# A graph attention kernel on Trainium2: SyncE fetches three search stretches out of four, one row a transfer, and GpSimd keeps the fourth

## The chip, the cores and the metric

One NeuronCore of one Trainium2 chip runs the whole kernel in one launch. The metric is the device time of one execution in microseconds (us). Engines carry the profile's short names: PE is TensorE, DVE is VectorE, ACT is ScalarE, POOL is GpSimd, SP is SyncE. SP has no arithmetic: it issues transfers (DMA) and waits. A name with a q (SPq) is the sequencer of that engine.

## The reference, cut to what matters

```python
h = x @ w_lin + b_lin                     # 12500 nodes, 64 features
msg = h[edge_src]                         # 400000 edges, sorted by edge_dst
counts = segment_sum(ones, edge_dst)      # edges of each node
starts = cumsum(counts) - counts          # where a node's edges begin
pos = arange(e) - starts[edge_dst]
dense[edge_dst, pos] = msg                # (12500, 32, 64), further edges dropped
mask[edge_dst, pos] = True
xb = mab(dense, dense, enc_*, mask)       # attention of a node's 32 slots among themselves
xp = relu(xb @ pma_lin_w + pma_lin_b)
p = mab(seed, xp, pma_*, mask)            # pooling to one vector a node
dd = mab(p, p, dec_*)                     # decoder
out = layernorm(x + relu(nan_to_num(dd)))
```

## The kernel before

**Work.** A slot is one of a node's 32 edges, a quad is 32 partitions, an octet is 32 nodes with their 1024 slots. There are 391 octets. Four octets are one iteration of 128 nodes, and there are 98 iterations (ITS). First a table of 12500 rows of 192 numbers (what the query, the feature and the value of a node come from) is computed and stored in DRAM as `node_table`; then the octets go through a software pipeline. All engines run `step(s)` for each octet number, written out for the first 16 steps, as a loop of 22 turns of PERIOD = 16 steps, and written out again for the tail. What an engine does in a step for an older or a younger octet is said by a lag (`L_FF = 4`: the octet four steps back; `AT_SEARCH = -6`: six steps ahead).

**Gathers.** In each step POOL issues eight indirect transfers at L547, each of which fetches 128 table rows into `gathered`, at the row numbers in `idx`. `gathered` has a ring of 8 octets; a step's gathers wait for `av_ps`, the attention product of the octet eight back. PE waits with L639 for the gathers of its octet.

**Search.** `idx` is found on the chip. For each iteration, DVE counts in `rows_of` (step lag AT_ROWS = -15) how many of 1250 samples of the sorted edge list lie below each of the 128 nodes (L908, `count_rows`), which gives for each node the row of `win_table` at which its edges begin. A row of `win_table` is a stretch of 352 edge targets and the same 352 edge sources, 2816 bytes. At lag AT_STRETCH = -8 POOL fetches the 128 rows of one iteration into `windows[:, buffer]` in one indirect transfer, `gather_windows` (L510), ahead of the step's eight gathers. At lag AT_SEARCH = -6 DVE waits for it in `landed`, and counts and shifts in the stretch in place; at lag -4 it writes `idx`. So the row numbers of an iteration are known seven steps before its stretch is fetched, and nine before it is searched. The first four iterations (DIRECT) are fetched another way, L517. There are two stretch buffers.

**SP.** SP loads inputs, stores the table, builds `win_table` (L476, L479), and then waits in L488 for the output parts, which are ready at the end. It does nothing between 67 us and 3919 us.

Of the kernel before, what the change touches and what calls it, by code (L numbers as in the profile page):

```python
# [25 lines left out]
ALU = mybir.AluOpType  # L26
# [22 lines left out]
STAGED = 16  # L49
DIRECT = 4  # L50
PERIOD = 16

# [26 lines left out]
class Step:  # L79
# [15 lines left out]
    def round(self, lag):  # L95
        return self.group * (PERIOD // RING) + (self.at - lag) // RING

    def slot(self, lag, n):
# [28 lines left out]
def gnn_kernel(nc, a, out):  # L127
# [33 lines left out]
    with ExitStack() as ctx:  # L161
# [19 lines left out]
        empty = sb("empty", [P, 512])  # L181
        consts = sb("consts", [P, 512])
        probs = sb("probs", [P, 2, 512])
# [34 lines left out]
        iota_j = sb("iota_j", [P, DEG])  # L218
        iota_ji = sb("iota_ji", [P, DEG], I32)
        node_i = sb("node_i", [P, ITS], I32)  # L220
        node_f = sb("node_f", [P, ITS])
# [21 lines left out]
        def c_(n, rows_=D):  # L243
# [4 lines left out]
        sample_i = sb("sample_i", [SAMPLE_ROWS, SAMPLE_TILES], I32)  # L248
        sample_f = sb("sample_f", [SAMPLE_ROWS, SAMPLE_TILES])
        sample_diag = xp_rows[0:SAMPLE_ROWS, :, :].rearrange("p s n -> p (s n)")[  # L250
            :, 24 * D:24 * D + SAMPLES].rearrange("p (k r) -> p k r", k=SAMPLE_TILES)
        ones = sb("ones", [SAMPLE_ROWS, P])
# [60 lines left out]
        x_in = [sem(f"x_in{i}") for i in range(6)]  # L313
        win_in = [sem(f"win_in{i}") for i in range(2)]
        found = sem("found")
# [64 lines left out]

        pe_passed, pool_passed, dve_passed = sem("pe_passed"), sem("pool_passed"), sem("dve_passed")

        block = ctx.enter_context(nc.Block())
# [62 lines left out]
        def _(sp):  # L446
# [35 lines left out]


            stores = 0
            for part, (lo, end) in enumerate(PARTS):
# [10 lines left out]
        def _(pool):  # L496
# [10 lines left out]
            one_where_zero(ident[:, :], [[-1, P]], 0)  # L507
            def gather_windows(u, buffer, at):
                wait_apart(pool, win_idx_ready, u - (DIRECT - 1), pool_passed)
                pool.indirect_dma_start(  # L510
                    out=windows[:, buffer, 0:2 * WIN], out_offset=None, in_=win_table,
                    in_offset=bass.IndirectOffsetOnAxis(ap=win_idx[:, at:at + 1], axis=0)).then_inc(win_in[buffer], 16)

            def gather_direct(u):
                pool.wait_ge(win_elem_ready, u + 1)
                for c, edges in enumerate((dst, src)):
                    pool.indirect_dma_start(  # L517
                        out=windows[:, u % 2, c * WIN:(c + 1) * WIN], out_offset=None,
                        in_=edges.rearrange("(n o) -> n o", o=1),
                        in_offset=bass.IndirectOffsetOnAxis(ap=win_elem[:, u:u + 1], axis=0)).then_inc(win_in[u % 2], 16)  # L520

# [6 lines left out]
            def step(s):  # L528
# [3 lines left out]
                if not s.looped and s.at in (0, 12 + AT_STRETCH):  # L532
                    u = 2 + (s.at > 0)
                    pool.wait_ge(idx_ready, u - 1)
                    gather_direct(u)
# [21 lines left out]
        def _(pe):  # L557
# [18 lines left out]
            for lo in range(0, SAMPLES, 512):  # L576
                hi = min(lo + 512, SAMPLES)
                pe.matmul(ps_samples[:, lo:hi], ones[:, :], flat[:, lo:hi], start=True, stop=True
                          ).then_inc(samples_ps, 1)
# [256 lines left out]
        def _(dve):  # L836
# [11 lines left out]
            V.memset(pma_diag[:, :], 0.0).then_inc(dve_zero, 1)  # L848
            V.memset(ones[:, :], 1.0)
            V.memset(consts[:, :], 0.0)  # L850
# [74 lines left out]

            def landed(u, half):

                direct = 2 if not isinstance(half, int) else min(half + 1, 2)
                dve.wait_ge(win_in[u], half * 16 + (16 + 16 * direct))

# [49 lines left out]
            for c in range(CHUNKS):  # L980
                table_odd(c)
                if c in (2, 4, 6):
                    elements_of(c // 2)
                if c == 8:
                    landed(0, 0)
                    search(0, 0, 0, 0)
                if c == 12:
                    landed(1, 0)
# [46 lines left out]

            iota_slots = iota_j[:, :].unsqueeze(1).broadcast_to((P, 2, DEG))

            def step(s):
# [135 lines left out]
                if s.has_iteration(AT_SEARCH) and (s.looped or s.at >= 8 + AT_SEARCH):  # L1174
                    u = s.iteration(AT_SEARCH)
                    par = s.slot(AT_SEARCH, RING) // OCTS_PER_IT
                    landed(par, s.round(AT_SEARCH))
                    count_edges(u, par, par)
                    shift(u, par, range(BITS - 1, SHIFTS - 1, -1))
                if s.has_iteration(AT_SHIFT) and (s.looped or s.at >= 8 + AT_SHIFT):  # L1180
                    par = s.slot(AT_SHIFT, RING) // OCTS_PER_IT
                    shift(s.iteration(AT_SHIFT), par, range(SHIFTS - 1, -1, -1))
# [3 lines left out]
                    index_of(par, s.slot(AT_SHIFT, PERIOD) // OCTS_PER_IT)  # L1186
                if s.has_iteration(AT_ROWS) and (s.looped or s.at >= 4 * DIRECT + AT_ROWS):
                    rows_of(s.iteration(AT_ROWS), s.slot(AT_ROWS, PERIOD) // OCTS_PER_IT)

# [93 lines left out]
```

## Time and profile before

| | |
|---|---|
| time, median of 3 runs | 4168.89 us (4167.66 to 4169.9) |
| the profiled execution | 4176.05 us, its span 4174.2 us |
| POOL | 3067.2 us busy, 73% of the span, 3236 instructions |
| PE | 3126.7 us, 75% |
| DVE | 3035.1 us, 73% |
| ACT | 1659.8 us, 40% |
| gathers L547 | 3125 |
| stretch gathers L510 | 94 |

Busy time counts executing alone. An engine whose instructions each need a fixed pause of issue behind them can be fully taken at 73% busy, so for each engine the reader has to look at what its idle time waited for. The span holds about 67 us of preparation, the pipeline, and a drain behind the last gather at 4108 us.

### The profile page before, as it was taken

How to read it: one execution, taken by the hardware profiler on the slowest of the kernel's cores; microseconds unless marked ns; L12 is line 12 of the kernel's file. 1: busy time of each engine (PE TensorE's matmuls, PEld its weight loads, DVE VectorE, ACT ScalarE, POOL GpSimd, SP SyncE). 2: the span in 40 equal slices, each digit the busy share in tenths (PEclk: the TensorE clock that was granted, in tenths of full speed). 3: DMA queues.
4: the chain of work that ended last, by engine and by line, in shares of the span. 5: the costliest groups of instructions: out<-in, count | busy, mean ns of one | idle time of the engine just before them, and what ended most of it. 6: DMA issues, size and time to landing. Idle time of an engine off the chain costs nothing.

```text
span 4174.2 us, 87208 instructions
## 1 busy us (share of the span) xinstructions
PE 3126.7 (75%) x30724; PEld 2000.1 (48%) x30724; DVE 3035.1 (73%) x7088; ACT 1659.8 (40%) x2990; POOL 3067.2 (73%) x3236
## 2 busy tenths in 40 slices
PE   5677777777777777777777777777777777777776
PEld 3444444454444444444444454444444444444444
DVE  4677777777777777777777777777776777777876
ACT  2343443444434434443444343443443444434443
POOL 3777777777777777777777777777777777777772
PEclk7898999999999999999999999999999999999998
DMA  5333333333333333333333333333333333333331
GB/s 197 87 85 88 85 88 84 87 88 85 87 86 87 85 88 85 87 85 88 85 87 86 87 85 88 85 87 85 88 87 85 88 85 87 85 88 85 97 95 35
DMA packets 170668, 368.55 MB, mean 88 GB/s; under 512 B 56190, under 2 KB 109094, under 8 KB 170230
## 3 DMA queue, kind: packets, MB, share of 16 engines
q0 software_dynamic: 158032, 342.73, 30.7%
q1 hardware_dynamic: 11877, 19.76, 1.3%
q8 instruction: 289, 4.73, 0.5%
q14 instruction: 150, 1.22, 0.1%
q10 hardware_dynamic: 320, 0.10, 0.0%
HBM read 349.58 MB, written 16.32 MB: 88 GB/s over the span
## 4 chain that ended last, share of the span: by engine, by line
POOL 63%; issue 21%; PE 7%; DMA 4%; DVE 3%; POOLq 1%; ACT 0%; SPq 0%; ACTq 0%; DVEq 0%
POOL gathered L547 61%; DMA gathered<-node_table,idx 4%; POOL windows L510 2%; PE ps L724 2%; PE ps L651 2%; PE ps L697 2%; DVE xb L1119 1%; PE ps L639 1%; DVE probs_diag L1193 0%; DVE flags L908 0%; POOLq L122 0%; PE ps L606 0%; POOLq L124 0%; PE ps L752 0%; DVE h L1075 0%
## 5 line engine op out<-in xcount | busy, mean ns | idle before, releaser
L547 POOL DMA_INDIRECT gathered<-node_table,idx x3125 | 2969.4, 950 | 952.4 <-issue 934.4
L639 PE MATMUL ps<-ident,gathered 128*128 128x128 f32 x3128 | 608.0, 326 | 748.7 <-DMA gathered<-node_table,idx 748.4
L639 PEld LDWEIGHTS ps<-ident,gathered 128*128 128x128 f32 x3128 | 501.7, 204 | 1104.8 <-issue 1062.8
L803 ACT ACTIVATE qT<-ps,cols 128x512 f32<-128x512 f32 x391 | 268.9, 688 | 1238.8 <-PE ps L639 1237.8
L1119 DVE SCALAR_TENSOR_TENSOR xb<-ps,cols,h 128x512 f32<-128x512 f32 x391 | 292.6, 748 | 640.6 <-PE ps L697 640.0
L761 ACT ACTIVATE h_apart<-ps 64x512 f32<-64x512 f32 x782 | 462.8, 592 | 443.7 <-PE ps L639 434.1
L1193 DVE STREAM_TRANSPOSE probs_diag<-probs 32x512 f32<-32x512 f32 x784 | 549.0, 700 | 18.3
L697 PE MATMUL ps<-h,ff_diag 128*128 128x512 f32 x782 | 505.6, 734 | 29.8 <-DVE h L1075 29.7
L651 PE MATMUL ps<-probs_diag,gathered 128*64 128x128 f32 x6256 | 449.4, 287 | 79.0 <-issue 78.6
L651 PEld LDWEIGHTS ps<-probs_diag,gathered 128*64 128x64 f32 x6256 | 363.3, 167 | 247.4 <-issue 230.9
L724 PE MATMUL ps<-xb,pma_diag 128*128 128x512 f32 x782 | 454.4, 664 | 31.3 <-DVE xb L1119 26.9
L683 PE MATMUL ps<-xp,seed_u 128*32 128x128 f32 x3128 | 431.1, 283 | 0.0
L761 ACT ACTIVATE xp_rows<-ps 128x512 f32<-128x512 f32 x391 | 233.5, 597 | 416.2 <-PE ps L675 415.6
L683 PEld LDWEIGHTS ps<-xp,seed_u 128*32 128x32 f32 x3128 | 318.7, 112 | 72.9 <-issue 68.8
L1075 DVE SCALAR_TENSOR_TENSOR h<-ps,cols,hT 128x512 f32<-128x512 f32 x391 | 290.5, 743 | 35.3 <-PE ps L651 35.3
L816 ACT ACTIVATE xp<-ps,cols 128x512 f32<-128x512 f32 x391 | 267.8, 685 | 97.7 <-PE ps L724 95.7
L961 DVE COPY_PREDICATED windows<-below_bits,windows 128x128 int32<-128x128 int32 (+8 forms) x882 | 211.9, 240 | 94.9 <-DVE windows L961 55.2
L675 PE MATMUL ps<-ident,xp 128*128 128x128 f32 x1564 | 252.5, 286 | 7.5 <-ACT xp L816 1.1
L761 ACT ACTIVATE hT<-ps 128x512 f32<-128x512 f32 x391 | 233.6, 597 | 9.8
L740 PEld LDWEIGHTS ps<-h_apart,qT 128*32 128x32 f32 x12544 | 189.7, 110 | 77.5 <-issue 76.0
L724 PEld LDWEIGHTS ps<-xb,pma_diag 128*128 128x128 f32 x782 | 122.9, 198 | 211.0 <-DVE xb L1119 106.2
L740 PE MATMUL ps<-h_apart,qT 128*32 128x64 f32 x12544 | 221.2, 222 | 1.5 <-ACT h_apart L761 1.4
(195 smaller groups left out, 3369.3 us busy)
## 6 DMA issues: line engine op xcount, KB each, us to landing
gathered<-node_table,idx POOLq DMA_INDIRECT x3125
node_table<-gathered SPq DMA_DIRECT2D x24, 384.0 KB, 2.8
out_rows<-rows SPq DMA_DIRECT2D x5, 416.0 KB
win_table<-in_dst SPq DMA_DIRECT2D x1, 1716.0 KB
win_table<-in_src SPq DMA_DIRECT2D x1, 1716.0 KB
windows<-win_table,win_idx POOLq DMA_INDIRECT x94, 3.7
rows<-in_x SPq DMA_DIRECT2D x2, 640.0 KB, 5.2
rows<-in_x SPq DMA_DIRECT2D x1, 768.0 KB, 7.2
```

The source lines that it names most:

```text
L547: pool.indirect_dma_start(out=gathered[:, s.slot(0, RING), t * ROW:(t + 1) * ROW], out_offset=None, in_=table, in_offset=bass.IndirectOffs ...
L639: mm = pe.transpose(ps[:, bank, p * P:(p + 1) * P], gathered[:, s.slot(0, RING), lo:lo + 2 * ROW - 2:3], ident[:, :])
L651: mm = pe.matmul(ps[D * h:D * h + D, B_AV, p * P:(p + 1) * P], gathered[:, s.slot(L_ATTEND, RING), lo:lo + ROW - 2:3], probs_diag[:, s.slo ...
L683: mm = pe.matmul(ps_seed[DEG * c:DEG * c + DEG, :], seed_u[:, 6 - 2 * p:38 - 2 * p], xp[:, s.slot(L_BACK, 2), p * P:(p + 1) * P], start=(p ...
L697: pe.matmul(ps[:, B_FF, :], ff_diag[:, :], h2[:, s.slot(L_FF, 2), :], start=True, stop=True).then_inc(ff_ps, 1)
L724: pe.matmul(ps[:, B_FF, :], pma_diag[:, :], xb[:, s.slot(L_PMA, 2), :], start=True, stop=True).then_inc(pma_ps, 1)
L740: mm = pe.matmul(ps[DEG * q:DEG * q + DEG, B_S + o, 2 * DEG * p:2 * DEG * (p + 1)], qT[:, s.slot(L_SCORES - o, 4), lo:lo + DEG], h_apart[: ...
L761: return nc.scalar.activation(o, i, ACT.Copy)
L803: nc.scalar.activation(qT[:, s.slot(0, 4), :], ps[:, B_Q, :], ACT.Identity, bias=c_("q_b", P)).then_inc(q_sb, 1)
L1075: V.scalar_tensor_tensor(h2[:, s.slot(L_H2, 2), :], ps[:, B_AV, :], c_("bo1", P), hT[:, s.slot(L_H2, RING), :], ALU.add, ALU.add).then_inc ...
L1119: V.scalar_tensor_tensor(xb[:, s.slot(L_FF, 2), :], ps[:, B_FF, :], c_("ff_b", P), h2[:, s.slot(L_FF, 2), :], ALU.add, ALU.max).then_inc(x ...
L1193: V.transpose(probs_diag[lo:lo + DEG, s.slot(L_NORM, 4) // 2, :, lo:lo + DEG], pr[lo:lo + DEG, :].rearrange("p (t j) -> p t j", j=DEG)).th ...
```

## The change

Of each four iterations, the one with `at == 0` is still fetched by POOL. The other three are fetched by SP: DVE transposes the column of 128 row numbers, so that the 32 numbers of a quad lie side by side in one partition (`odd_turned`); SP loads each quad's 32 numbers into registers, and issues for each a transfer of one row of `win_table` into one partition of `windows`. Each is a DMA with an address from a register. Four stretch buffers take the place of two, and DVE waits on four semaphores (one a quad) for a stretch of SP. To make room, `flags` are bf16 and some tiles share memory. In all 70 of the 94 stretches move to SP, in 23 turns of a loop of three stretches and one more behind it, and all ahead of the output stores in SP's order.

```diff
@@ sync
+            def odd_rows(b, count):
+
+                wait_apart(sp, odd_turned_ready, count, sp_passed)
+                for q in range(QUADS):
+                    _, at = nc.values_load_multi_w_load_instructions(
+                        odd_turned[DEG * q:DEG * q + 1, b, :], engines=(mybir.EngineType.SP,), min_val=0,
+                        max_val=SAMPLES - 1, skip_runtime_bounds_check_because="a count of the samples, less one")
+                    for j in range(DEG):
+                        sp.dma_start(windows[DEG * q + j:DEG * q + j + 1, 1 + b, 0:2 * WIN],
+                                     win_table[bass.ds(at[j], 1), :]).then_inc(odd_in[b][q], 16)
+
+            sp.wait_ge(table_in, 64)
+            with sp.Fori(0, (ITS - 6) // 4) as turn:
+                for k in range(3):
+                    odd_rows(k, turn * 3 + k + 1)
+            odd_rows(0, (ITS - 6) // 4 * 3 + 1)
@@ gpsimd
-            def gather_windows(u, buffer, at):
-                wait_apart(pool, win_idx_ready, u - (DIRECT - 1), pool_passed)
+            def gather_windows(s):
+                wait_apart(pool, win_idx_ready, s.period(AT_STRETCH), pool_passed)
+                at = s.slot(AT_STRETCH, PERIOD) // OCTS_PER_IT
                 pool.indirect_dma_start(
-                    out=windows[:, buffer, 0:2 * WIN], out_offset=None, in_=win_table,
-                    in_offset=bass.IndirectOffsetOnAxis(ap=win_idx[:, at:at + 1], axis=0)).then_inc(win_in[buffer], 16)
+                    out=windows[:, 0, 0:2 * WIN], out_offset=None, in_=win_table,
+                    in_offset=bass.IndirectOffsetOnAxis(ap=win_idx[:, at:at + 1], axis=0)).then_inc(win_in[0], 16)
@@ gpsimd, step
-                if s.has_iteration(AT_STRETCH) and (s.looped or s.at >= 16 + AT_STRETCH):
+                if s.has_iteration(AT_STRETCH) and s.slot(AT_STRETCH, PERIOD) == 0 and (s.looped or s.at >= 16 + AT_STRETCH):
                     wait_apart(pool, idx_ready, s.iteration(AT_STRETCH) - 1, pool_passed)
                     if not s.looped and s.at == 16 + AT_STRETCH:
                         pool.wait_ge(table_in, 64)
-                    at = s.slot(AT_STRETCH, PERIOD) // OCTS_PER_IT
-                    gather_windows(s.iteration(AT_STRETCH), at % 2, at)
+                    gather_windows(s)
@@ vector
-            def rows_of(u, at):
-
+            def rows_of(s):
+
+                u = s.iteration(AT_ROWS)
+                at = s.slot(AT_ROWS, PERIOD) // OCTS_PER_IT
                 count_rows(u, at, u + 1)
-                V.tensor_scalar(win_idx[:, at:at + 1], win_row[:, at:at + 1], -1.0, None, ALU.add).then_inc(win_idx_ready, 1)
+                minus = V.tensor_scalar(win_idx[:, at:at + 1], win_row[:, at:at + 1], -1.0, None, ALU.add)
+                if at == 0:
+                    minus.then_inc(win_idx_ready, 1)
+                else:
+                    n = s.period(AT_ROWS) * 3 + (at - 3)
+                    minus.then_inc(odd_idx_ok, 1)
+                    wait_apart(dve, odd_idx_ok, n, dve_passed)
+                    V.transpose(odd_turned[:, at - 1, :], win_idx[:, at:at + 1].broadcast_to((P, DEG))
+                                ).then_inc(odd_turned_ready, 1)
@@ vector, landed(s)
+                at = s.slot(AT_SEARCH, PERIOD) // OCTS_PER_IT
+                if at:
+                    for q in range(QUADS):
+                        dve.wait_ge(odd_in[at - 1][q], s.period(AT_SEARCH) * (16 * DEG))
+                else:
+                    dve.wait_ge(win_in[0], s.period(AT_SEARCH) * 16 + 32)
+                return at
@@ memory
-        windows = sb("windows", [P, 2, 2 * WIN + DEG], I32)
+        windows = sb("windows", [P, 4, 2 * WIN + DEG], I32)
-        flags = [sb(f"flags{i}", [P, n]) for i, n in enumerate((SAMPLES, WIN, WIN))]
+        flags = [sb(f"flags{i}", [P, n], BF16) for i, n in enumerate((SAMPLES, WIN, WIN))]
```

On POOL, this stands before in the first eight of the 16 steps of the loop (`L122` is a register instruction of a wait; eight gathers are one step; line numbers here are those of the file before):

```order
L122 REGISTER_ALU
L510 DMA windows<-win_table,win_idx 128x704
L122 ISA
L547 DMA gathered<-node_table,idx 128x192 x8
L122 REGISTER_ALU
L547 DMA gathered<-node_table,idx 128x192 x8
L122 REGISTER_ALU
L547 DMA gathered<-node_table,idx 128x192 x8
L122 REGISTER_ALU
L547 DMA gathered<-node_table,idx 128x192 x8
L122 REGISTER_ALU x2
L510 DMA windows<-win_table,win_idx 128x704
```

In the changed kernel (where L571 is the gather and L537 the stretch gather) the only stretch gather of POOL's loop stands behind the eighth step of a turn:

```order
L571 DMA gathered<-node_table,idx 128x192 x8
L126 REGISTER_ALU
L571 DMA gathered<-node_table,idx 128x192 x8
L126 REGISTER_ALU x2
L537 DMA windows<-win_table,win_idx 128x704
L126 REGISTER_ALU
L571 DMA gathered<-node_table,idx 128x192 x8
```

So a turn of 16 steps has 128 gathers and one stretch gather on POOL, where it had 128 and four.

On SP, the transfers that build `win_table` (L488 here) are followed by the new loop, whose L505 is its head, L497 the load of 32 row numbers into registers, each ISA at L501 the address arithmetic of one row, and each DMA at L501 one row:

```order
L488 DMA win_table<-in_src 2x352
L505 UNCONDITIONAL_BRANCH
L505 ISA
L497 TENSOR_LOAD odd_turned
L501 ISA
L501 DMA windows<-win_table 1x704
L501 ISA
L501 DMA windows<-win_table 1x704
```

Before, the output stores followed directly there. Now a stretch is four loads and 128 pairs of ISA and DMA, and the stores stand behind the last stretch.

## Rows read from the trace of the kernel before

**Rows 1.** The page: span, busy time, and the chain that ended last.

```profile
span 4174.2 us, 87208 instructions
...
PE 3126.7 (75%) x30724; PEld 2000.1 (48%) x30724; DVE 3035.1 (73%) x7088; ACT 1659.8 (40%) x2990; POOL 3067.2 (73%) x3236
...
POOL 63%; issue 21%; PE 7%; DMA 4%; DVE 3%; POOLq 1%; ACT 0%; SPq 0%; ACTq 0%; DVEq 0%
POOL gathered L547 61%; DMA gathered<-node_table,idx 4%; POOL windows L510 2%; PE ps L724 2%; PE ps L651 2%; PE ps L697 2%; DVE xb L1119 1%; PE ps L639 1%; DVE probs_diag L1193 0%; DVE flags L908 0%; POOLq L122 0%; PE ps L606 0%; POOLq L124
```

**Rows 2.** Waits of POOL: us in total, times, longest us.

```profile
POOL gathered L547 <- issue: 934.4, 3066, 0.3
POOL windows L510 <- issue: 28.6, 94, 0.3
POOL gathered L547 <- PE ps L651: 18.0, 59, 0.3
```

**Rows 3.** Timeline of POOL: start us, us, what, idle before it.

```profile
2010.56 0.95 POOL L510 DMA_INDIRECT windows<-win_table,win_idx  x1 [0.31 <-issue]
2011.81 0.95 POOL L547 DMA_INDIRECT gathered<-node_table,idx  x1 [0.30 <-issue]
```

**Rows 4.** Lines L510, L547: count, ns min/median/max, first and last start.

```profile
L510 POOL DMA_INDIRECT windows<-win_table,win_idx x94: 942/947/1031, 150.5 to 3999.3; - x94
...
L547 POOL DMA_INDIRECT gathered<-node_table,idx x3125: 942/947/1892, 67.8 to 4108.4; - x196
```

**Rows 5.** Busy time of each engine in 16 steps of the loop.

```profile
core 0: us, PE busy (x) PEld busy (x) DVE busy (x) ACT busy (x) POOL busy (x), PEclk, DMA share, GB/s
2010.50:2176.00 165.50, 124.89 (x1244) 80.61 (x1244) 121.67 (x285) 66.79 (x120) 125.30 (x132) 0.93 0.32 86
```

**Rows 6.** Waits of all engines: PE for the gathers.

```profile
PE ps L639 <- DMA gathered<-node_table,idx: 748.4, 321, 10.1
```

**Rows 7.** Line L953 on VectorE, a transpose of 128x32.

```profile
L953 DVE STREAM_TRANSPOSE count_turned<-count x98: 198/203/329, 30.9 to 4037.9; 128x32 f32<-128x32 f32 x98
```

**Rows 8.** Issues of SP by line, ns min/median/max.

```profile
L488 SPq DMA_DIRECT2D out_rows<-rows x8: 332/332/357, 3919.1 to 4171.6; - x8
...
L453 SPq DMA_DIRECT2D rows<-in_x x5: 371/432/529, 3.9 to 5.8; - x5
...
L464 SPq DMA_DIRECT2D node_table<-gathered x24: 325/532/2212, 19.5 to 60.8; - x24
...
L479 SPq DMA_DIRECT2D win_table<-in_dst x1: 659/659/659, 63.7 to 63.7; - x1
L479 SPq DMA_DIRECT2D win_table<-in_src x1: 2011/2011/2011, 65.0 to 65.0; - x1
```

**Rows 9.** Timeline of SP: three issues.

```profile
59.69 0.53 SPq L464 DMA_DIRECT2D node_table<-gathered  x1
60.27 0.47 SPq L460 DMA_DIRECT2D cols<-in_L_gnn_dec_out_b  x1
60.84 0.53 SPq L464 DMA_DIRECT2D node_table<-gathered  x1
```

**Rows 10.** Sequencer instructions by line, ns min/median/max.

```profile
L908 DVEq FUSED_REGOPS  x88: 46/53/57, 260.6 to 3858.8; - x88
...
L389 PEldq COMPARE_BRANCH  x22: 83/3688/4318, 404.8 to 3879.5; - x22
...
L124 POOLq EVENT_SEMAPHORE  x616: 17/17/17, 218.1 to 3846.4; - x154
```

**Rows 11.** DMA queues: packets, MB, share of 16 DMA engines.

```profile
q0 software_dynamic: 158032, 342.73, 30.7%
q1 hardware_dynamic: 11877, 19.76, 1.3%
```

**Rows 12.** Waits of SP: us in total, times, longest us.

```profile
SPq L488 <- DVE rows L1256: 4102.2, 8, 3852.1
```

More of the change, by code:

```diff
@@ L50 @@
 DIRECT = 4
+DIRECT_BUFFER = (0, 1, 2, 3)
 PERIOD = 16
@@ L96, in round, with period @@
         return self.group * (PERIOD // RING) + (self.at - lag) // RING
+    def period(self, lag):
+        return self.group + (self.at - lag) // PERIOD
     def slot(self, lag, n):
@@ L181, in gnn_kernel @@
         empty = sb("empty", [P, 512])
-        consts = sb("consts", [P, 512])
+        consts = sb("consts", [P, 2 * P])
         probs = sb("probs", [P, 2, 512])
@@ L248, in gnn_kernel @@
         sample_i = sb("sample_i", [SAMPLE_ROWS, SAMPLE_TILES], I32)
-        sample_f = sb("sample_f", [SAMPLE_ROWS, SAMPLE_TILES])
+        sample_f = lnv[0:SAMPLE_ROWS, 0, 0:SAMPLE_TILES]
         sample_diag = xp_rows[0:SAMPLE_ROWS, :, :].rearrange("p s n -> p (s n)")[
             :, 24 * D:24 * D + SAMPLES].rearrange("p (k r) -> p k r", k=SAMPLE_TILES)
-        ones = sb("ones", [SAMPLE_ROWS, P])
-        flags = [sb(f"flags{i}", [P, n]) for i, n in enumerate((SAMPLES, WIN, WIN))]
+        ones = pool_part[0:SAMPLE_ROWS, 0:P]
+        flags = [sb(f"flags{i}", [P, n], BF16) for i, n in enumerate((SAMPLES, WIN, WIN))]
+        odd_turned = sb("odd_turned", [P, 3, DEG], I32)
         win_row = sb("win_row", [P, 4])
@@ L257, in gnn_kernel @@
         win_elem = sb("win_elem", [P, DIRECT], I32)
-        windows = sb("windows", [P, 2, 2 * WIN + DEG], I32)
+        windows = sb("windows", [P, 4, 2 * WIN + DEG], I32)
+        node_i = windows[:, 3, 0:ITS]
+        iota_ji = windows[:, 3, ITS:ITS + DEG]
         below = sb("below", [P, 1])
@@ L313, in gnn_kernel @@
         x_in = [sem(f"x_in{i}") for i in range(6)]
-        win_in = [sem(f"win_in{i}") for i in range(2)]
+        win_in = [sem(f"win_in{i}") for i in range(4)]
+        odd_in = [[sem(f"odd_in{b}{q}") for q in range(QUADS)] for b in range(3)]
+        odd_idx_ok = sem("odd_idx_ok")
+        odd_turned_ready = sem("odd_turned_ready")
         found = sem("found")
@@ L517, in gather_direct @@
                     pool.indirect_dma_start(
-                        out=windows[:, u % 2, c * WIN:(c + 1) * WIN], out_offset=None,
+                        out=windows[:, DIRECT_BUFFER[u], c * WIN:(c + 1) * WIN], out_offset=None,
                         in_=edges.rearrange("(n o) -> n o", o=1),
-                        in_offset=bass.IndirectOffsetOnAxis(ap=win_elem[:, u:u + 1], axis=0)).then_inc(win_in[u % 2], 16)
+                        in_offset=bass.IndirectOffsetOnAxis(ap=win_elem[:, u:u + 1], axis=0)).then_inc(win_in[DIRECT_BUFFER[u]], 16)
             for u in range(2):
@@ L577, in _ @@
                 hi = min(lo + 512, SAMPLES)
-                pe.matmul(ps_samples[:, lo:hi], ones[:, :], flat[:, lo:hi], start=True, stop=True
+                pe.matmul(ps_samples[:, lo:hi], ones, flat[:, lo:hi], start=True, stop=True
                           ).then_inc(samples_ps, 1)
@@ L848, in _ @@
             V.memset(pma_diag[:, :], 0.0).then_inc(dve_zero, 1)
-            V.memset(ones[:, :], 1.0)
+            V.memset(ones, 1.0)
             V.memset(consts[:, :], 0.0)
@@ L924, in elements_of, with direct_landed, landed @@
                                 ).then_inc(win_elem_ready, 1)
-            def landed(u, half):
-                direct = 2 if not isinstance(half, int) else min(half + 1, 2)
-                dve.wait_ge(win_in[u], half * 16 + (16 + 16 * direct))
+            def direct_landed(u):
+                b = DIRECT_BUFFER[u]
+                dve.wait_ge(win_in[b], 32 * DIRECT_BUFFER[0:u + 1].count(b))
+            def landed(s):
+                u = s.iteration(AT_SEARCH)
+                if not s.looped and u < DIRECT:
+                    direct_landed(u)
+                    return DIRECT_BUFFER[u]
+                at = s.slot(AT_SEARCH, PERIOD) // OCTS_PER_IT
[5 more added lines that the diff above has]
+                return at
             def search(u, h, buffer, at):
@@ L984, in _ @@
                 if c == 8:
-                    landed(0, 0)
+                    direct_landed(0)
                     search(0, 0, 0, 0)
                 if c == 12:
-                    landed(1, 0)
+                    direct_landed(1)
                     search(1, 1, 1, 1)
@@ L1036, in _ @@
             iota_slots = iota_j[:, :].unsqueeze(1).broadcast_to((P, 2, DEG))
+            searched = [0]
             def step(s):
@@ L1176, in step @@
                     par = s.slot(AT_SEARCH, RING) // OCTS_PER_IT
-                    landed(par, s.round(AT_SEARCH))
-                    count_edges(u, par, par)
-                    shift(u, par, range(BITS - 1, SHIFTS - 1, -1))
+                    searched[0] = landed(s)
+                    count_edges(u, par, searched[0])
+                    shift(u, searched[0], range(BITS - 1, SHIFTS - 1, -1))
                 if s.has_iteration(AT_SHIFT) and (s.looped or s.at >= 8 + AT_SHIFT):
-                    par = s.slot(AT_SHIFT, RING) // OCTS_PER_IT
-                    shift(s.iteration(AT_SHIFT), par, range(SHIFTS - 1, -1, -1))
+                    shift(s.iteration(AT_SHIFT), searched[0], range(SHIFTS - 1, -1, -1))
                     for lag in (12, 11, 10, 9):
@@ L1185, in step @@
                             dve.wait_ge(g_in[s.slot(lag, RING)], s.round(lag) * (16 * OCT) + 16 * OCT)
-                    index_of(par, s.slot(AT_SHIFT, PERIOD) // OCTS_PER_IT)
+                    index_of(searched[0], s.slot(AT_SHIFT, PERIOD) // OCTS_PER_IT)
                 if s.has_iteration(AT_ROWS) and (s.looped or s.at >= 4 * DIRECT + AT_ROWS):
-                    rows_of(s.iteration(AT_ROWS), s.slot(AT_ROWS, PERIOD) // OCTS_PER_IT)
+                    rows_of(s)
             def to_diagonal(s, pr, first, last):
```

7 lines of the change are left out of this document (2 added, 5 removed).

## The prediction

> **What bounds the kernel now.** I read the chain that ended last first. POOL's instructions are 63% of it and "issue" another 21%, nearly all of it the gathers of L547 [rows 1]. The waits of POOL say what that issue time is: 3066 of the 3125 gathers waited for nothing that the profile shows, 0.3 us each, and where PE's L651 is named, the wait is the same 0.3 us at most [rows 2]. The timeline shows the beat: a gather starts every 1.25 us, 0.95 executing and 0.30 of issue, and a stretch gather of L510 takes exactly one beat between two of them [rows 3]. So 73% busy is a full engine. From the first and last start of L510, 93 intervals of 33 beats lie in 3848.8 us [rows 4]: 41.385 us an iteration, **1.254 us a beat**, 165.5 us a turn of 16 steps (132 beats). In such a turn PE is busy 124.9 us and DVE 121.7 us [rows 5], and PE waits 748.4 us in all for landed gathers [rows 6], 1.9 us for each of 391 octets. The other engines have room; SP sleeps (its longest wait 3852.1 us [rows 12]).
>
> **What the change takes away.** 70 of the 94 beats of L510 leave POOL. 70 x 1.254 = **87.8 us**. A turn is then 129 beats, 161.8 us. The steps without a stretch gather already run at 8 beats, so nothing else is asked to be faster than it has been for three steps out of four.
>
> **What it adds on DVE.** For each of 70 stretches a 128x32 transpose, 0.20 us by the row of another one [rows 7], a wait of one DVE instruction for another (some 0.1 us) and three more semaphore waits: about 0.4 us, 1.2 us of a turn in which DVE has 40 free. It hides behind PE's wait for gathers [rows 6]; with that cover gone it would cost 70 x 0.4 = 28 us. bf16 flags change no count of instructions; I take nothing.
>
> **What it adds on SP, the term that decides.** A turn has three stretches: 384 row issues, each behind one fused register instruction, 12 register loads, a few waits, and one branch. The pieces:
> - Register instruction: 46 to 57 ns on DVE [rows 10]; I take 46.
> - The pause between two SP instructions: 60.27 - 59.69 - 0.53 = 0.05 us; with a semaphore wait in between, 60.84 - 60.27 - 0.47 = 0.10 [rows 9]. So 0.045 a pause, two a row. The row costs its issue + 0.136 us.
> - Register load of 32 words: no row. The nearest is a whole issue, 0.33 us [rows 8]; with its pause 12 x 0.375 = 4.5 us a turn. Below it is a register instruction (12 x 0.09 = 1.1); above I take one such instruction a word, 32 x 0.046 = 1.5 us, 18 us a turn.
> - Branch back: 3.7 us by PE's, whose loop is also long [rows 10]. Waits and counters: 0.5.
> - Sum: 384 x (issue + 0.136) + 8.7 us a turn.
>
> SP keeps up if this is below 161.8, that is **if an issue takes at most 0.263 us**; it costs more than before (165.5) above 0.272. Now the issues of the trace [rows 8]: alone, 128 rows on an idle SP, 0.325 to 0.332; close behind another 0.43 to 0.53; behind a transfer of 1248 rows 0.659 and 2.011. The last ones show that part of an issue grows with the size of the job ahead. None of the trace moves one row. An issue cannot be less than a semaphore instruction, 0.017 [rows 10], and the shortest seen is 0.325. The nearest row is the 0.33, with which SP would lose. I still take **0.25**: each of those issues starts 128 rows over all DMA engines, the new one starts a single contiguous piece, so that there is no job ahead to wait for and less to set up. That a quarter of 0.33 is such set-up is my choice, not a reading. With it a turn is 384 x 0.386 + 8.7 = **156.9 us**, 4.9 under POOL's 161.8, and SP is 97% taken. The first such stretch has nine steps (91 us) from its row numbers to its search; three in a row, at 52 us each, leave the third ready 157 - 80 = 77 us after its numbers, still early.
>
> The Trainium skill prices a register load as a "`tensor_load` floor" of about 600 ns (DMA: Bandwidth & Descriptors, Latency and other measured facts); by it, as an estimate, the loads are 7.7 us a turn in place of 4.5, and the sum is 160.1, just inside. No row here shows a load.
>
> **DMA.** The bytes are the same, 2816 a row. At the software queue's rate, 30.7% of 16 engines x 4174.2 us for 342.73 MB [rows 11], 59.8 us of one engine a MB, a row is 0.168 us; by the hardware queue's 1.3% for 19.76 MB it is 0.12. Spread over 16 engines that is nothing new. If all 128 rows went through one engine, it would have 21.5 us of them in 53.9 us, 40%, beside the 31% of the gathers: 71%. The gathers' landing may come a few tenths later; PE's 1.9 us an octet covers it. [...]
>
> **The drain.** The output stores stand behind the last stretch in SP's order. That stretch is needed by octet 388, some 9 steps before the pipeline's end, and seven of eight stores have no reader. Nothing.
>
> **Sum.** 4176.05 - 87.8 = 4088.3 for the profiled execution, which is 0.17% above the median; at the median 4168.9 - 87.8 = 4081. I say 4082.
>
> **Rivals.**
> - *SP becomes the bound, slower than before.* One mechanism: the issue of one row costs as much as that of 128. For it speaks that 0.325 is the shortest of all and the same at eight stores of different width. The end is then DVE waiting in `landed`, and behind it `idx`, POOL and PE. At 0.332 the turn is 384 x 0.468 + 8.7 = 188.4 us, 22.9 more than before, x 23.3 turns = +534: **4703**. At 0.30: 176.1, +247: 4416. At the 0.532 of back-to-back issues: 265.2, +2326: 6495. It decides from 0.272 us. Chance 0.29.
> - *Loads word by word.* With 0.25 for the issue but 1.5 us a load: 148.2 + 18.5 + 4.2 = 170.9, +5.4 a turn, +126: **4295**. It decides from 1.1 us a load. The Trainium skill gives some 200 ns a register for a load from HBM (Runtime: NRT & Kernel Launch, Instruction fetch mechanics); the estimate by it is 6.4 us a load and a turn of 229 us, 1480 us more. Chance 0.06.
> - *One DMA engine fills up.* If a row holds it for 0.35 us in place of 0.17, 128 x 0.35 + 16.7 = 61.5 us a stretch, 184.5 a turn, +443: **4612**. It decides from 0.30 us a row. Chance 0.03.
> - *Just at the edge.* An issue of 0.263 to 0.272: POOL's gain is eaten by SP, 4082 to 4169. Chance 0.05, 0.03 of it within the bound of no change.
> - *The forecast.* 4076 to 4092. Chance 0.57.
>
> **How the numbers follow.** Faster by over 0.2% (what can be told from no change here, 8 us): 0.57 + 0.02 = 0.59. Within: 0.03. Slower: 0.29 + 0.06 + 0.03 = 0.38. The cases lie on both sides. The range takes in the forecast, the edge, the word-by-word case, and the first rival up to its 0.332 us: 4075 to 4710; beyond it stay the dearer issues. The likeliest case's own range is 4076 to 4092.
>
> **What would show it.** Right: 24 stretch gathers on POOL, the beat still 1.25 us, POOL's waits still "issue", row issues of SP under 0.26 us, SP waiting for `odd_turned` a little in each stretch, and no wait of DVE at `landed`. Wrong: row issues at 0.3 us or more back to back without a wait of SP, long waits of DVE at the first count of a search (L941 before) for a transfer, POOL waiting for `idx`, and PE for it. A load longer than 1.1 us, or gathers that land later than before, would show the two smaller rivals.

## The result: slower by 12.3%

The changed kernel takes 4681.31 us (median of 4 runs, 4678.71 to 4682.61), the kernel before 4168.64 us on the same chip (4 runs, 4167.66 to 4169.9): a ratio of 1.1229, 95% interval [1.1209, 1.1248], 512.7 us more. The forecast of 4082 us is wrong in its sign; the time lies in the range, close to the first rival's 4703. The profiled execution took 4682.61 us.

The page of the changed kernel, with the chain that ended last and the queues, where [rows 1, 11] had POOL at 73% busy and 63% of the chain:

```profile
span 4680.8 us, 114667 instructions
...
PE 3046.6 (65%) x30724; PEld 1961.6 (42%) x30724; DVE 3044.4 (65%) x7158; ACT 1673.5 (36%) x2990; POOL 2992.1 (64%) x3166
...
q0 software_dynamic: 152432, 317.49, 25.7%
q1 hardware_dynamic: 29797, 45.03, 3.2%
...
SPq 68%; issue 26%; POOL 3%; PE 1%; DVE 1%; DMA 0%; ACT 0%; ACTq 0%; POOLq 0%; DVEq 0%
```

SP, which slept before, is 68% of the chain, and "issue" (mostly its own pauses) another 26%. The other engines do the work they did, in a longer span. POOL is 75 us less busy: 66 of them are the 70 stretch gathers that it lost (70 x 0.947), the other 9 are gathers of L571 that last 3 ns less in the mean. The two queues together take 28.9% of the DMA engines, where they took 32.0%. PE's mean granted clock fell from 0.912 to 0.855, but PE is busy 3046.6 us where it was 3126.7, so its matmuls did not get longer in sum.

What SP executes, by line of the changed kernel (L501 is the row's transfer, L497 the register load, L505 the loop; count, ns min/median/max, first and last start):

```profile
L501 SPq FUSED_REGOPS  x8960: 37/37/43, 141.7 to 4548.1; - x200
L501 SPq MOVE windows<-win_table x8960: 29/29/38, 141.8 to 4548.2; - x200
L501 SPq DMA_DIRECT2D windows<-win_table x8960: 224/225/304, 141.8 to 4548.2; - x200
...
L497 SPq TENSOR_LOAD <-odd_turned x280: 2029/2119/2291, 139.6 to 4532.9; - x140
...
L505 SPq ALU_OP  x23: 37/37/37, 325.9 to 4486.2; - x23
```

Three readings. The issue of one row is 0.225 us, below even the chosen 0.25. A load of 32 registers is 2.12 us, where the forecast had 0.33 (each with a pause behind it). And there is a third instruction a row, a MOVE, which the forecast did not have. The loop's counter instruction stands once in each of 23 passes: (4486.2 - 325.9) / 22 = **189.1 us a turn**, where POOL needs 161.8.

A stretch of SP's timeline (start us, us, what):

```profile
1701.57 4.35 SPq L501 DMA_DIRECT2D windows<-win_table  x11
```

Eleven rows, taken from the first one's MOVE to the last one's issue, last 4.35 us. Ten beats and the last row's MOVE, pause and issue (0.029 + 0.031 + 0.225) make that, so a row is 0.407 us. One such beat in the chain (start us, us, what): the issue of a row, the register instruction, the MOVE and the next issue, with a pause before each:

```profile
2000.17 0.23 SPq L501
2000.40 0.05 issue
2000.45 0.04 SPq L501
2000.48 0.04 issue
2000.52 0.03 SPq L501
2000.55 0.03 issue
2000.58 0.23 SPq L501
```

Who waits now (us in total, times, longest us):

```profile
PE ps L721 <- DVE h L1124: 1225.2, 227, 28.9
DVE flags L988 <- DMA windows<-win_table: 978.6, 45, 26.9
POOL gathered L571 <- issue: 939.1, 3080, 0.3
POOL gathered L571 <- DVE idx L1014: 460.0, 31, 22.2
...
PE ps L663 <- DMA gathered<-node_table,idx: 80.3, 25, 9.8
```

L988 is the first count of a search: DVE waits there for the rows, POOL waits for the `idx` that DVE then writes late, and PE's wait for gathers has shrunk from 748.4 us [rows 6] to 80.3, because PE now stands behind DVE instead (L721, 1225.2 us). SP itself waits for nothing but the start and the end:

```profile
SPq L514 <- DVE rows L1304: 124.8, 2, 111.4
SPq L128 <- DVE odd_turned L948: 59.0, 1, 59.0
```

One wait for row numbers in the whole execution, the first one. An engine whose input is always ready is the bound.

**The turn in pieces.** 384 rows x 0.407 = 156.3 us; 12 loads x 2.12 = 25.4; the rest of the 189.1, 7.4 us, is the pauses at loads and waits, the branch and longer pauses now and then. The largest single piece of it is the pause behind the branch back to the loop's head, once a turn:

```profile
2028.34 2.73 issue
```

### The profile page after: what moved, and what is told of

Its sections match the earlier page's. It is cut to its first block, busy times and chain, and to the rows that moved or that the text cites. A ratio compares the mean times of both kernels' runs of the same rounds, so it can differ in the third digit from the quotient of the medians.

```text
span 4680.8 us, 114667 instructions
## 1 busy us (share of the span) xinstructions
PE 3046.6 (65%) x30724; PEld 1961.6 (42%) x30724; DVE 3044.4 (65%) x7158; ACT 1673.5 (36%) x2990; POOL 2992.1 (64%) x3166
## 3 DMA queue, kind: packets, MB, share of 16 engines
q0 software_dynamic: 152432, 317.49, 25.7%
## 4 chain that ended last, share of the span: by engine, by line
SPq 68%; issue 26%; POOL 3%; PE 1%; DVE 1%; DMA 0%; ACT 0%; ACTq 0%; POOLq 0%; DVEq 0%
SPq L501 55%; SPq L497 12%; POOL gathered L571 3%; PE ps L630 0%; PE ps L721 0%; DVE flags L932 0%; PE ps L776 0%; DVE probs_diag L1241 0%; DVE windows L1008 0%; DVE gathered L1023 0%; DMA gathered<-node_table,idx 0%; PE ps L734 0%; PE ps L748 0%; PE ps L602 0%; PE ps L663 0%
## 5 line engine op out<-in xcount | busy, mean ns | idle before, releaser
L571 POOL DMA_INDIRECT gathered<-node_table,idx x3125 | 2960.7, 947 | 1403.4 <-issue 939.1
L721 PE MATMUL ps<-h,ff_diag 128*128 128x512 f32 x782 | 474.3, 691 | 1227.6 <-DVE h L1124 1225.2
L988 DVE TENSOR_SCALAR_CACHE_REDUCE flags<-windows,node_f 128x352 bf16<-128x352 int32 x98 | 55.8, 570 | 978.6 <-DMA windows<-win_table 978.6
L721 PEld LDWEIGHTS ps<-h,ff_diag 128*128 128x128 f32 x782 | 128.8, 207 | 1269.2 <-issue 1247.6
L663 PEld LDWEIGHTS ps<-ident,gathered 128*128 128x128 f32 x3128 | 468.3, 200 | 383.1 <-issue 382.2
L663 PE MATMUL ps<-ident,gathered 128*128 128x128 f32 x3128 | 554.6, 303 | 80.4 <-DMA gathered<-node_table,idx 80.3
```

The source lines that it names most:

```text
L571: pool.indirect_dma_start(out=gathered[:, s.slot(0, RING), t * ROW:(t + 1) * ROW], out_offset=None, in_=table, in_offset=bass.IndirectOffs ...
L663: mm = pe.transpose(ps[:, bank, p * P:(p + 1) * P], gathered[:, s.slot(0, RING), lo:lo + 2 * ROW - 2:3], ident[:, :])
L721: pe.matmul(ps[:, B_FF, :], ff_diag[:, :], h2[:, s.slot(L_FF, 2), :], start=True, stop=True).then_inc(ff_ps, 1)
```

## The experiments

Three theories. **A**: SP's own instructions set the time, each with its pause: a row is the issue (0.225), the register instruction (0.037), the MOVE (0.029) and three pauses (0.116 together), and a load is 2.12. **B**: the price is that of issuing a row, as the first rival had it, and the rest lies beside it (in the expectation of `one_reg`, B is something else: a load costs the same whatever its words). **C**: the transfers fill a DMA engine or a queue, and SP is held up. After the second set came **D**: a kernel that fetches the same stretches again and again makes its gathers read the same table rows many times over, and that slows the gathers. Each ratio is against the kernel before on the same chip, which took 4168.03 us on one and 4178.94 us on another.

### First set

Four edits were timed on a chip on which the kernel before took 6393.44 us in place of 4169. In the trace of `static` there, PE's small matmuls (L761) waited for issue 1582 times, 1731.7 us in all, and DVE behind them another 1932.3 us. What SP costs can hide behind such waits, so the ratios say next to nothing of the change. All four were run again.

> The changed kernel, but each register load fetches one number in place of 32, and the 32 rows of a quad all come from that number's row, so the stretches hold other edges. Theory A, SP's own instructions set the end and a load costs by the word: 2.12 us a load falls to some 0.4, a turn of SP from 189.1 to 384 x 0.408 + 12 x 0.45 + 6.2 = 168.3 us; from the changed kernel's 4681 us 22 turns x 20.8 less, about 4225 us, still a little over the kernel before (4169). Theory B, a load costs by the instruction whatever its words: 4681, no change. Theory C, the end is set by the transfers, which all go through few DMA engines beside the gathers: 4681, no change, with DVE waiting as long for the rows while SP sleeps between stretches.

Measured: 6423.12 us, ratio 1.0047 [1.003, 1.0064].

> The changed kernel without register loads, and each row fetched from a fixed row of the table, so that the 8960 transfers of 2816 bytes stay and the address work goes; the stretches hold other edges. Theory A, SP's instructions: a row costs issue and pause, 0.225 + 0.045 us, a turn of SP 384 x 0.27 + 6 = 110 us, far under POOL's 161.8, so the whole gain is there: 4169 - 88 = 4081 us, SP asleep for 50 us a turn. Theory C, the transfers: as many, as large and to the same places, so 4681 us or at least over 4300.

Measured: 6402.1 us, ratio 1.0016 [1.0006, 1.0026].

> All of the work is done. DVE multiplies the row number by 2816 in the instruction that subtracts one, and SP uses the loaded number as a byte address, so the fused register instruction of each row is gone (0.037 us and its pause of 0.051). Theory A: a row falls from 0.408 to 0.320 us, a turn of SP to 384 x 0.320 + 12 x 2.15 + 6.2 = 154.9 us, under POOL's 161.8: the gain appears, 4083 us (4076 to 4100). If the move before each issue goes too, 132 us and the same time. Theory C: 4681, no change.

Measured: 6411.64 us, ratio 1.0024 [1.0012, 1.0035].

> All of the work is done. SP fetches two stretches of four, POOL the other two. Theory A: SP needs 2 x 60.8 + 5 = 127 us a turn, POOL 130 beats of 1.254, 163.0 us; 47 beats leave POOL, 4169 - 59 = 4110 us. Theory C: SP's transfers fill a share of two thirds of what they did; if they held 189 us a turn before, they hold 126, and the time is 4110 too, so this run tells the sizes and not the theories apart. Over 4169 would say that rows by SP slow something else.

Measured: 6501.16 us, ratio 1.0168 [1.0151, 1.0185].

### Without the register instruction

DVE multiplies the row number into a byte address, and SP addresses the table as bytes, so that it has nothing to work out:

```diff
-            minus = V.tensor_scalar(win_idx[:, at:at + 1], win_row[:, at:at + 1], -1.0, None, ALU.add)
+            minus = V.tensor_scalar(win_idx[:, at:at + 1], win_row[:, at:at + 1], -1.0, float(8 * WIN), ALU.add, ALU.mult)
...
-            win_table[bass.ds(at[j], 1), :]
+            table_bytes[:, bass.ds(at[j], 8 * WIN)]
```

> The kernel of the run bytes again, on a chip where the kernel before takes its 4169 us; on the other chip every version stood between 6393 and 6502 us, held up by PE's issue. DVE multiplies the row number by 2816 in the instruction that subtracts one, and SP uses the loaded number as a byte address: no register instruction a row. Theory A, SP's own instructions set the end: a row falls from 0.408 to 0.320 us, a turn of SP from 189.1 to 154.9 us, under POOL's 161.8: 4083 us (4076 to 4100). Theory C, the transfers set it: 4681, no change.

Measured: 4089.34 us (4078.97 to 4089.92) against 4178.94 (4176.69 to 4180.09), ratio **0.9787 [0.9771, 0.9804]**, span 4077.2 us, within A's 4076 to 4100. This is the fastest of the versions that do all the work. Page, SP by line, and waits:

```profile
POOL 69%; issue 23%; PE 3%; DVE 2%; DMA 1%; POOLq 1%; ACT 0%; SPq 0%; ACTq 0%; DVEq 0%
...
L504 SPq MOVE windows<-win_table x8960: 29/29/53, 138.1 to 3900.5; - x200
L504 SPq DMA_DIRECT2D windows<-win_table x8960: 222/225/345, 138.1 to 3900.6; - x200
...
L500 SPq TENSOR_LOAD <-odd_turned x280: 2036/2122/2196, 136.0 to 3888.0; - x140
...
L508 SPq ALU_OP  x23: 37/37/37, 287.7 to 3840.8; - x23
...
PE ps L666 <- DMA gathered<-node_table,idx: 657.3, 297, 10.2
...
SPq L129 <- DVE odd_turned L955: 215.4, 23, 58.7
```

The FUSED_REGOPS of the rows are gone, nothing else: same rows, same transfers, same loads. POOL is 69% of the chain, SP 0%. SP now waits for its row numbers once a turn, (215.4 - 58.7) / 22 = 7.1 us each time. A turn is (3840.8 - 287.7) / 22 = 161.5 us, POOL's, so SP works 154.4: 34.7 less than in the changed kernel, 384 x **0.090 us**. A register instruction of 37 ns costs 90 with its pause. B is out (the issues are still 0.225), and so is C: the same 8960 transfers in a shorter span stop nobody.

### Two stretches of four

```diff
-                for k in range(3):
-                    odd_rows(k, turn * 3 + k + 1)
+                for k in range(2):
+                    odd_rows(2 * k, turn * 2 + k + 1)
```

GpSimd fetches the other two of four groups; the row has all three instructions.

> The kernel of the run two_of_four again: SP fetches two stretches of four. Theory A: SP needs 127 us a turn, POOL 130 beats, 163.0 us: 4169 - 59 = 4110 us. On the other chip this version stood 1.7% above the kernel before; if it does here too, rows by SP slow something that my sum has not.

Measured: 4119.6 us (4117.84 to 4120.16), ratio 0.986 [0.9843, 0.9876], span 4116.0. SP's waits:

```profile
SPq L128 <- DVE odd_turned L948: 795.9, 44, 19.7
...
L505 SPq ALU_OP  x23: 37/37/37, 280.7 to 3867.8; - x23
```

SP waits 44 times, 795.9 / 22 = 36.2 us of each turn of (3867.8 - 280.7) / 22 = 163.1, so it works 126.9, where A had 127. 47 gathers taken from POOL x 1.254 = 58.9 us, and 4178.94 - 4119.6 = 59.3 were gained. So [rows 4]'s price of a gather on POOL holds, and with SP below its limit the change pays what it removes.

### Fewer instructions a row, and the same rows for each stretch

`one_reg` loads one number for 32 rows and fetches that row for all of them:

```diff
-                        odd_turned[DEG * q:DEG * q + 1, b, :], engines=(mybir.EngineType.SP,), min_val=0,
+                        odd_turned[DEG * q:DEG * q + 1, b, 0:1], engines=(mybir.EngineType.SP,), min_val=0,
...
-                                     win_table[bass.ds(at[j], 1), :]).then_inc(odd_in[b][q], 16)
+                                     win_table[bass.ds(at[0], 1), :]).then_inc(odd_in[b][q], 16)
```

`static` has no load at all:

```diff
-                    _, at = nc.values_load_multi_w_load_instructions(
...
-                                     win_table[bass.ds(at[j], 1), :]).then_inc(odd_in[b][q], 16)
+                                     win_table[DEG * q + j:DEG * q + j + 1, :]).then_inc(odd_in[b][q], 16)
```

> The kernel of the run one_reg again: each load fetches one number, which serves the 32 rows of its quad (the stretches hold other edges). The other chip's trace has such a load at 0.525 us against 2.12 for 32 numbers. Theory A: a turn of SP is 384 x 0.408 + 12 x 0.56 + 6.2 = 169.6 us, 19.5 less than 189.1, x 22 = 429 less than 4681: about 4250 us. Theory C: 4681.

Measured: 5778.34 us (5772.94 to 5794), ratio 1.3834, span 5780.5.

> The kernel of the run static again: no register loads, each row from a fixed row of the table (the stretches hold other edges), 8960 transfers as before. Theory A: SP needs about 110 us a turn, POOL is the bound again at 161.8: 4081 us. Theory C: 4681, or at least over 4300.

Measured: 5527.07 us (5521.26 to 5534.4), ratio 1.3234, span 5519.4. Less work for SP, and 850 to 1100 us more: no theory had that. (The trace of `one_reg_b` has 280 register instructions in place of 8960, so its rows had still less to do than expected.) The page and SP's line of `static_b`:

```profile
q0 software_dynamic: 152432, 317.49, 64.0%
...
SPq 83%; issue 10%; POOL 4%; PE 1%; DVE 1%; DMA 1%; ACT 0%; POOLq 0%; ACTq 0%; DVEq 0%
...
L498 SPq DMA_DIRECT2D windows<-win_table x8960: 211/244/2734, 137.0 to 5354.9; - x200
```

The gathers' queue moves the same 152432 packets and 317.49 MB as in the changed kernel, but they hold the DMA engines for 64.0% of the span in place of 25.7%, and some issues of SP last 2.7 us in place of 0.24. The median issue is still 0.244 us; in the chain, 83% of 5519 us over 8960 issues is a mean of 0.51. That is C's mechanism, SP held up by DMA engines with more to do, but is it the rows or the gathers that fill them? Both kernels search stretches that needn't hold the node, so other numbers come out in `idx`, and the gathers read other rows of the node table. That these repeat is D. From the same set, a price that stands: `one_reg_b` loads one number a time.

```profile
L497 SPq TENSOR_LOAD <-odd_turned x280: 439/525/592, 136.3 to 5613.7; - x140
```

0.525 us for one number, 2.12 for 32: (2.12 - 0.525) / 31 = 0.051 us a further number. So a load is priced by the word, which answers the B of `one_reg`.

### The same rows, with gathers that stay spread

`static_b` again, but the gathers of SP's groups read fixed, distinct node numbers:

```diff
+            V.tensor_copy(idx[:, 1:4, :].rearrange("p a j -> p (a j)"), node_f[:, 0:3 * DEG])
...
-                V.transpose(idx[:, at, :], src_win[:, 0:DEG])
+                V.transpose(windows[:, buffer, 0:DEG] if at else idx[:, at, :], src_win[:, 0:DEG])
```

> Left out: no loads and no register addresses, each row number j fetches row j of the table of stretches, and the gathers of the three groups read 96 fixed columns of distinct node numbers instead of the search's result. It differs from the earlier kernel with fixed rows by these node numbers alone. Theory A: a row costs 0.286 us, 384 of them 110 us a turn, SP waits, GpSimd's 129 beats set the turn again: 4081 us, ratio 0.979. Theory D (the earlier kernel was slow because the search of wrong stretches made every gather read the same row of the node table): 4081 us, the software queue back from 64% to about 29%, no issue of a row above 0.4 us. Theory C (rows that SP fetches from the same places again and again, or its 0.29 us beat, fill the queues): stays at about 5500 us with the queue at 64%.

Measured: 4078.09 us (4075.83 to 4081.55) against 4168.03 (4166.24 to 4171.91, 7 runs), ratio 0.9786 [0.977, 0.9803], span 4076.1.

```profile
q0 software_dynamic: 152432, 317.49, 29.1%
...
L498 SPq DMA_DIRECT2D windows<-win_table x8960: 211/243/497, 137.4 to 3888.4; - x200
...
1700.01 1.10 SPq L498 DMA_DIRECT2D windows<-win_table  x4
...
1700.01 6.12 SPq L498 DMA_DIRECT2D windows<-win_table  x20
...
SPq L128 <- DVE odd_turned L945: 1089.9, 67, 59.3
```

1449 us come back by other numbers in `idx` alone (the two runs are from two chips, 11 us apart in the kernel before), at the same instructions and transfers of SP. The first four of these rows take 1.10 us, (1.10 - 0.243) / 3 = 0.286 from start to start; all twenty take 6.12, 0.309 with the longer pauses among them. With a queue at 29% they don't hold anyone up. So C is out for the rows, and A's figure, 4081, is met. The longest issue was 0.497 us; none above 0.4 was expected.

### One node row for all gathers, on the kernel before

```diff
+            V.memset(idx[:, 1:4, :], 0)
...
-                V.transpose(idx[:, at, :], src_win[:, 0:DEG])
+                V.transpose(windows[:, buffer, 0:DEG] if at else idx[:, at, :], src_win[:, 0:DEG])
```

> The kernel before, with GpSimd fetching all stretches; left out: the result of the search is not used for three groups out of four, whose gathers all read row 0 of the node table (indices set to zero once). All searches and all gathers run. Theory D (gathers of one repeated row are slow, whoever fetches the stretches): the software queue goes from 31% to 60% or more, TensorE waits for gathers, and the time goes to 5300 to 5600 us though SP has nothing to do with it. Theory C (the slowness belongs to SP's rows): 4169 us.

Measured: 5058.8 us (5051.75 to 5067.33), ratio 1.2133 [1.2112, 1.2153].

```profile
q0 software_dynamic: 158032, 342.73, 78.5%
```

In [rows 11] the same packets and bytes took 30.7%. SP has nothing to do with it here. D holds in kind and not in size (5300 to 5600 was expected): the slowdown of the gathers is a thing of its own; that `static_b` and `one_reg_b` lose still more, though their share is lower, fits SP's issues being held up as well, but no run separates that part.

### A quarter of the loads

With the gathers spread in the same way, the numbers of the first quad only are loaded. A different factor for each quad keeps one register instruction and one MOVE for each row:

```diff
-                    _, at = nc.values_load_multi_w_load_instructions(
+                    if q == 0:
+                        _, at = nc.values_load_multi_w_load_instructions(
...
-                        win_table[bass.ds(at[j], 1), :]
+                        table_elems[:, bass.ds(at[j] * (2 * WIN - 16 * q), 2 * WIN)]
```

> Left out: the row numbers of three quads in four are not loaded; their rows are fetched from places worked out of the first quad's registers (row number times 704, 688, 672 or 656 words), and the gathers of the three groups read 96 fixed columns of distinct node numbers in place of the search's result, so that the gathered rows stay spread over the table. Kept: 96 rows a turn for each quad, one register instruction and one MOVE a row, all searches, all gathers. Theory A (SP's own instructions set the time; a load of 32 words costs 2.12 us and a pause of 0.03): nine loads of twelve go, 9 x 2.15 = 19.4 us of the 189.1 us turn, which leaves 169.7 us, still above GpSimd's 161.8 and above the 165.5 of before; 68 stretches x 6.45 us = 439 us less than the change: 4242 us, about 1.017 of before. Theory B (the price is the issue of the row, the loads lie beside transfers or issues): 4681 us. Theory D (my fixed node numbers disturb nothing): the share of the software queue stays near 26 to 29%.

Measured: 4230.27 us (4184.36 to 4233.89), ratio 1.0117 [1.0057, 1.0176], span 4228.3 (three of the four runs lie within 4 us of each other, the fourth is 46 us lower).

```profile
SPq 64%; issue 29%; POOL 3%; PE 2%; DVE 1%; DMA 0%; ACT 0%; ACTq 0%; POOLq 0%; DVEq 0%
...
L500 SPq TENSOR_LOAD <-odd_turned x70: 2038/2043/2078, 139.0 to 4033.4; - x70
...
L508 SPq ALU_OP  x23: 37/37/37, 305.6 to 4033.2; - x23
```

A turn is (4033.2 - 305.6) / 22 = 169.4 us; A had 169.7, and 4242 for the whole, where B had 4681. Nine loads are worth 189.1 - 169.4 = 19.7 us, 2.19 each: nothing of a load is hidden. SP is still the bound, still above 165.5.

### Each load twice

> Nothing left out: the changed kernel with each load of 32 row numbers issued twice. Theory A: twelve more loads a turn, 12 x 2.15 = 25.8 us, a turn of 214.9 us, 68 x 8.6 = 585 us more than the change: 5266 us. Theory B (a load is hidden behind issues or transfers in flight): 4681 us. If the second load of a pair is cheaper because the first is still under way, its mean says so and the sum falls by it.

Measured: 4677.95 us (4677.66 to 4679.57), ratio 1.1224. It tests nothing: the profile has the 280 loads and the 114667 instructions of the changed kernel. All 280 are of L500, the load that the rows use; of L497, the added first load of each pair, whose registers no one reads, there is none. It is a repetition, on a later occasion, and shows how well the time of the changed kernel repeats: 3.4 us apart.

## Why the prediction was wrong

**What bounded the kernel before, and what the change takes away:** right. POOL's beat of 1.254 us and the 87.8 us for 70 gathers are met by `bytes_b` (4178.94 - 4089.34 = 89.6) and `static_spread` (4168.03 - 4078.09 = 89.9); the turn of 161.8 is 161.5.

**DVE's additions:** right, nothing. In `bytes_b` they are all there, PE still waits 657.3 us for gathers, and the time is POOL's.

**SP, the term that decides:** this step failed. The prediction had a turn of 156.9 us, 4.9 under POOL; it is 189.1, 32.2 more. By its own pieces:
- *The issue of a row*, 0.25 by choice and against the nearest row: 0.225. The choice was on the right side, 384 x 0.025 = 9.6 us to the good. That a single contiguous piece is cheaper to issue than 128 rows over all engines is what the rows of the trace after show.
- *The row around it*, "two pauses and one register instruction, 0.136": 0.182. One register instruction was read from the listing of the program, but the hardware profile has a FUSED_REGOPS and a MOVE, and three pauses. 384 x 0.046 = 17.7 us to the bad. The sum for a row is 0.407 in place of 0.386: +8.1 us.
- *The load of 32 registers*, "a whole issue, 0.33, with its pause 0.375": 2.12. 12 x 1.79 = **+21.5 us**, the largest part of the miss. This was the term mis-sized: the range put between a register instruction and 1.5 us did not reach it, since its upper end counted 0.046 us a word and nothing for the start. Measured, it is 0.525 for the first and 0.051 for each further word. The upper end's price per word was nearly right; it was the middle that was taken, not the end.
- The remainder, some 2.6 us, is pauses and waits. The branch itself is not in it: with 2.73 us it is below the 3.7 of the sum.

Would one of the two errors alone have turned the sign? From the measured 189.1: with loads at 0.33 the turn is 167.6, 2.1 above before; without the MOVE and its pause (384 x 0.06 = 23.0) it is 166.1, 0.6 above. Each estimate is still above 165.5; no run took out the MOVE alone. `load_once`, with nine of twelve loads gone, measures 169.4 and is slower than before. So the forecast put SP at 97% of POOL's turn by a sum to which the trace adds a fifth (32.2 to 156.9 us), and with either of the two terms as wrong as it was there is no gain.

**The first rival** ("SP becomes the bound") is what happened, its chain of waits included: DVE at the first count of a search, `idx`, POOL, PE. But its mechanism, an issue of one row as dear as that of 128, is not what the trace shows (0.225, not 0.332). Its turn of 188.4 us is near 189.1 by accident: 0.107 us too much a row, against 0.046 too little around it and 1.79 too little a load. That the measured time lies in the stated range is the same luck, since this rival set its upper end. **The second rival** ("loads word by word") named the mechanism of the largest part of the miss; at 0.046 us a word it put 1.5 us on a load, and with 0.25 for the issue and no MOVE it gave 4295. With the measured 2.12 in its sum the turn is 148.2 + 12 x 2.165 + 4.2 = 178.4, about 4470: the right sign, but short of 4681, as the MOVE and the third pause are not in it. Its chance of 0.06 was too small for a term that no row showed.

**Register loads by the skill.** The Trainium skill states a "`tensor_load` floor" of about 600 ns (DMA: Bandwidth & Descriptors, Latency and other measured facts). The trace of `one_reg_b` has 0.525 us for a load of one number from SBUF, 0.439 the shortest, so here it is no floor in the strict sense, and the measured 0.525 stands. It says nothing of 32 words in one instruction; the estimate of 160.1 us a turn took it for the whole price, and so it too came out just inside. The some 200 ns a register that the Trainium skill gives for a load from HBM (Runtime: NRT & Kernel Launch, Instruction fetch mechanics) is four times the 0.051 measured here for SBUF, but as the only one of the two that grew with the number of registers it was the warning.

**One DMA engine fills up:** not in the changed kernel. The hardware queue has 17920 packets more than before, two for each of the 8960 rows, so a row's data went as one packet. The queue's share is of 16 engines: 3.2% x 16 x 4680.8 = 2397 us of engine time, less the 868 of before (1.3% x 16 x 4174.2), is about 0.17 us a row, as the prediction had it by the software queue, and this rival needed 0.30. Even if all rows went through one engine (the profile does not say which they used), they would hold it for a third of the span. In `bytes_b` the same rows cost no one a wait.

**The drain:** right, nothing: `bytes_b`, with the stores in the same order, meets the sum without it.

## What to carry to other kernels

Before work moves to an idle sequencer, count its instructions as the hardware profile would name them, with some 0.03 to 0.05 us of pause behind each: at 384 rows a turn one MOVE of 29 ns and its pause come to some 23 us by the estimate above, more than the whole margin. Address arithmetic belongs on an engine that does 128 of them at once: one multiplication moved to DVE turned +12.3% into -2.1%. And a sum that clears its limit by 3% with one term not in the trace is not a forecast of a gain; its price should be looked for in both directions, per instruction and per word.

When an experiment changes what a gather reads its addresses from, look first at the addresses; keep them spread, or its time tells of the gathers and not of the edit.

## What was not expected of the hardware

- A register load of 32 words takes 2.12 us and of one word 0.525 us, and nothing of it is hidden (nine fewer a turn gave back 2.19 us each).
- The issue of one contiguous row of 2816 bytes takes 0.225 us, against 0.325 for 128 rows [rows 8], and with a fixed address 0.243. Of 8960 of them the longest was 0.304 us in the changed kernel, 0.345 in `bytes_b` and 0.497 in `static_spread`, with the software queue at 26 to 29% of the DMA engines, and 2.7 us in `static_b`, where it held 64%.
- A transfer whose address comes from a register brings a MOVE of 29 ns of its own; with a fixed address there is none.
- Gathers of one repeated row of the table hold the DMA engines longer than spread ones, for the same packets and bytes (`same_node`, with three groups of four on one row: 78.5% of 5065.5 us against 30.7% of 4174.2, 3976 against 1281 us, a factor of 3.1).
- On one chip the kernel before and all four edits timed there took 6393 to 6501 us. Why was not looked into.
